# Mixing attention units two of a kind, one slot on, in a four-layer grid network

## What is computed

```python
def _L2_conv_ref(x, wq, bq, wk, bk, wv, bv):
    xf = x.reshape(B, N, C)          # N = 1024, C = 128; q and k have 16 channels
    q = xf @ wq + bq
    k = xf @ wk + bk
    v = xf @ wv + bv
    attn = jax.nn.softmax(jnp.einsum('bnd,bmd->bnm', q, k), axis=-1)
    out = jnp.einsum('bnm,bmc->bnc', attn, v)
    return out.reshape(B, H, W, C) + x
```

## Time and profile before

| | us |
|---|---|
| median of 3 runs | 4534.51 (4533.5 to 4537.09) |
| profiled execution, its own time | 4535.49 |
| its span, first to last instruction | 4533.4 |
| mean granted clock of TensorE, share of full speed | 0.986 |

### The profile page before, as it was taken

How to read it: one execution, slowest core, us unless ns; L and a number is a source line. 1 busy time by engine, 2 the same in 40 slices (tenths; PEclk the granted TensorE clock), 3 DMA queues, 4 the chain that set the end, 5 groups by cost and what they waited for, 6 DMA issues and landing times.

```text
span 4533.4 us, 56308 instructions
## 1 busy us (share of the span) xinstructions
PE 4349.7 (96%) x16776; PEld 2252.3 (50%) x16776; DVE 3476.5 (77%) x6544; ACT 2842.2 (63%) x5235; POOL 2267.5 (50%) x3972
## 2 busy tenths in 40 slices
PE   6989996999999999999999999999999999999996
PEld 2446654444444444444444444444444444446754
DVE  5988876777777777777777777777777775898876
ACT  1323322788888888888888888888888884333321
POOL 4654431455555555555555555555555556564431
PEclk9999998899999999999999999999999999999998
DMA  9869419111111122222211111112222221679429
GB/s 165 96 69 109 94 28 67 42 59 60 60 60 56 55 69 70 70 71 71 67 61 59 60 60 60 55 55 67 69 71 71 71 65 33 64 85 121 86 37 47
DMA packets 482495, 309.68 MB, mean 68 GB/s; under 512 B 420624, under 2 KB 432272, under 8 KB 482192
## 3 DMA queue, kind: packets, MB, share of 16 engines
q1 hardware_dynamic: 479088, 305.03, 35.2%
q10 hardware_dynamic: 3104, 1.06, 0.2%
HBM read 137.21 MB, written 135.27 MB: 60 GB/s over the span
## 4 chain that ended last, share of the span: by engine, by line
PE 64%; DVE 9%; ACT 8%; issue 8%; POOL 7%; SPq 2%; DMA 0%; DVEq 0%; POOLq 0%; ACTq 0%
PE psum L1158 14%; PE psum L1078 7%; PE psum L1129 6%; PE psum L1068 6%; PE psum L1092 5%; POOL probs_low L597 4%; PE psum L1142 3%; PE psum L1166 3%; PE psum L1164 3%; PE psum L1163 3%; PE psum L1201 3%; PE psum L1179 3%; PE psum L1188 3%; ACT shared L972 3%; PE psum L1087 3%
## 5 line engine op out<-in xcount | busy, mean ns | idle before, releaser
L597 POOL TENSOR_TENSOR probs_low<-shared,probs_high 128x512 fp32r<-128x512 f32 x1024 | 1307.4, 1277 | 1300.2 <-DVE probs_high L907 1300.2
L869 DVE TENSOR_REDUCE top<-psum 128x1 f32<-128x1024 f32 x1024 | 1253.9, 1225 | 616.1 <-PE psum L1142 615.8
L977 ACT ACTIVATE psum<-psum,top 128x1024 f32<-128x1024 f32 x1024 | 1114.9, 1089 | 279.6 <-DVE top L869 279.6
L972 ACT ACTIVATE shared<-psum 128x512 f32<-128x512 f32 x2048 | 1108.3, 594 | 258.9 <-PE psum L1129 258.8
L1158 PE MATMUL psum<-shared 128*128 128x512 f32 x2048 | 1123.6, 630 | 0.9 <-issue 0.5
L962 ACT ACTIVATE shared<-psum,b_col 128x320 f32<-128x320 f32 (+10 forms) x744 | 413.6, 567 | 1009.5 <-PE psum L1078 995.0
L588 POOL TENSOR_TENSOR shared<-arena 128x32 f32<-128x32 f32 (+6 forms) x1230 | 588.7, 509 | 764.8 <-PE psum L1078 725.2
L1163 PE MATMUL psum<-probs_high,v_high 128*128 128x512 f32 x1024 | 811.5, 792 | 0.0
L1068 PE MATMUL psum<-arena,w_own 128*128 128x320 f32 (+12 forms) x1672 | 539.5, 450 | 21.6 <-DVE w2wy L713 20.8
L1078 PE MATMUL psum<-shared,w_sum 128*128 128x320 f32 (+10 forms) x1488 | 523.3, 474 | 28.7 <-POOL shared L588 13.7
L1129 PE MATMUL psum<-q,k 64*128 64x512 f32 x2048 | 513.2, 497 | 0.3 <-ACT shared L972 0.3
(11 more groups left out here) (115 smaller groups left out, 4455.1 us busy)
## 6 DMA issues: line engine op xcount, KB each, us to landing
layer_out<-x SPq DMA_DIRECT2D x128, 512.0 KB, 2.6
x<-layer_out SPq DMA_DIRECT2D x124, 512.0 KB, 3.3
q<-q SPq DMA_DIRECT2D x256, 128.0 KB, 2.3
arena<-layer_out SPq DMA_DIRECT2D x63, 241.5 KB, 2.4
arena<-x_cells SPq DMA_DIRECT2D x6, 1520.0 KB, 12.3
layer_out<-arena SPq DMA_DIRECT2D x6, 1520.0 KB, 21.1
arena<-layer_out SPq DMA_DIRECT2D x6, 1520.0 KB, 10.9
y_cells<-arena SPq DMA_DIRECT2D x6, 1520.0 KB, 21.4
```

The source lines that it names most:

```text
L597: nc.gpsimd.tensor_tensor(probs_low[n % 2][:], probs[u % PROBS], probs_high[n % 2][:], ALU.subtract).then_inc(probs_split, 1)
L869: nc.vector.reduce_max(top[i % 2][:, m:m + 1], rows_ps[m % 2][:], AX_X, negate=True).then_inc(row_max, 1)
L972: nc.scalar.activation(probs[u % PROBS], keys_ps[u % 2], ACT.Exp).then_inc(probs_ready, 1)
L977: nc.scalar.activation(rows_ps[m % 2][:], rows_ps[m % 2][:], ACT.Exp, bias=top[i % 2][:, m:m + 1], accum_out=total[i % 2][:, m:m + 1]).the ...
```

## The change

Units are mixed two of a kind. The units of an even slot (u // 2 even) are mixed in fp32, both; those of an odd slot in three passes, both. Mixing is still one slot behind, so TensorE mixes in fp32 in odd slots and in passes in even slots. In a pass slot the four products with high parts come first, then the two with low parts. The casts and subtractions of a pair stand together in the odd slots. Value tiles are dealt out anew so that `v` (fp32) and `v_high`, `v_low` hold what their units need. `project_keys` moves from slot 6, before the mix, to slot 5, behind it; the query split on VectorE and the swap on SP from slot 7 to slot 0 of the next turn, `low_values` to slot 4; the shift's last three operations before its rounding go to a function of their own in slot 3 (`log_corrections`), the rest of `shift_values` to slot 4. No product, cast or subtraction is added or removed. The core of the diff:

```diff
+def in_passes(u):
+    return u // 2 % 2 == 1
...
+def split_index(i, u):
+    return UNITS // 2 * i + 2 * (u // 4) + u % 2
...
@@ SP
+                    if s == 0:
+                        swap_queries(j + 2)
...
-                    if s == 7:
-                        swap_queries(j + 3)
@@ GpSimd
-                split_probs(j, 2 * s + 1)
                 if s == 2:
                     log_sums(j + 1)
                 if s == 3:
+                    log_corrections(j + 1)
+                if s == 4:
                     shift_values(j + 1)
+                if in_passes(2 * s):
+                    split_probs(j, 2 * s)
+                    split_probs(j, 2 * s + 1)
@@ VectorE
-            row_maximum(j + 1 + (s + 6) // MT, (s + 6) % MT)
+            if s == 0:
+                split_queries(j + 2)
             if s == 2:
                 guess_log(j + 1)
-            if s == 3:
+            if s == 4:
                 low_values(j + 1)
+            row_maximum(j + 1 + (s + 6) // MT, (s + 6) % MT)
             if s == 5:
                 take_shift(j + 1)
             if s == 6:
                 split_keys(j + 3)
-            if s == 7:
-                split_queries(j + 3)
-            round_probs(j, 2 * s + 1)
+            if in_passes(2 * s):
+                round_probs(j, 2 * s)
+                round_probs(j, 2 * s + 1)
@@ ScalarE
             exponentials(j, 2 * s)
-            exponentials(j, 2 * s + 1)
             if s == 2:
                 shrink_sums(j + 1)
+            exponentials(j, 2 * s + 1)
@@ TensorE
+        def mix_whole(i, first):
...
+            for u in (first, first + 1):
                 pe.wait_ge(probs_ready, UNITS * i + u + 1)
-                nc.tensor.matmul(mix_ps, v[i % 2][:, t], probs[u % PROBS], start=(m == 0), stop=False
+                nc.tensor.matmul(mix_ps, v[i % 2][:, value_rows(u)], probs[u % PROBS], start=(u % MT == 0), stop=False
                                  ).then_inc(mixed, 1)
...
+        def mix_passes(i, first):
...
+            for u in (first, first + 1):
+                pe.wait_ge(probs_rounded, split_index(i, u) + 1)
+                nc.tensor.matmul(mix_ps, v_high[i % 2][:, value_rows(u)], probs_high[u % 2][:], start=False, stop=False)
+                nc.tensor.matmul(mix_ps, v_low[i % 2][:, value_rows(u)], probs_high[u % 2][:], start=False, stop=False)
+            for u in (first, first + 1):
+                pe.wait_ge(probs_split, split_index(i, u) + 1)
+                nc.tensor.matmul(mix_ps, v_high[i % 2][:, value_rows(u)], probs_low[u % 2][:], start=False,
+                                 stop=(u % MT == MT - 1)).then_inc(mixed, 1)
...
-            if s == 6:
-                project_keys(j + 3)
             if s == 7:
                 project_queries(j + 3)
-            for u in (2 * s - 2, 2 * s - 1):
-                mix(j + u // UNITS, u % UNITS)
+            i, first = j + (2 * s - 2) // UNITS, (2 * s - 2) % UNITS
+            if in_passes(first):
+                mix_passes(i, first)
+            else:
+                mix_whole(i, first)
+            if s == 5:
+                project_keys(j + 3)
```

More of the change, by code:

```diff
@@ L311, in tile, with value_tiles @@
     return slice(m * P, (m + 1) * P)
+def in_passes(u):
+    return u // 2 % 2 == 1
+def split_index(i, u):
+    return UNITS // 2 * i + 2 * (u // 4) + u % 2
+def value_tiles(h):
+    return [g * MT // 2 + p for p in range(h, MT // 2, 2) for g in range(2)]
 def queries_at(g, h):
@@ L594, in split_probs @@
             if is_job(i):
-                n = UNITS // 2 * i + u // 2
+                n = split_index(i, u)
                 pool.wait_ge(probs_rounded, n + 1)
@@ L614, in log_sums, with log_corrections @@
             nc.gpsimd.tensor_tensor(slope[:], slope[:], excess[:], ALU.mult).then_inc(log_turn, 1)
+        def log_corrections(i):
+            if not is_job(i):
+                return
+            turn = LOG_TURNS * i + 6
+            pool.wait_ge(log_turn, turn)
+            nc.gpsimd.tensor_scalar(slope[:], slope[:], -0.5, None, ALU.add).then_inc(log_turn, 1)
+            nc.gpsimd.tensor_tensor(log_sum[:], log_sum[:], excess[:], ALU.subtract).then_inc(log_turn, 1)
+            pool.wait_ge(log_turn, turn + 2)
+            nc.gpsimd.tensor_tensor(slope[:], slope[:], square[:], ALU.mult).then_inc(log_turn, 1)
         def shift_values(i):
@@ L621, in shift_values @@
             high, low = shift[i % 2][:, 0:MT], shift[i % 2][:, MT:2 * MT]
[L622 to L626, removed]
             pool.wait_ge(log_turn, turn + 3)
@@ L903, in round_probs @@
             if is_job(i):
-                n = UNITS // 2 * i + u // 2
+                n = split_index(i, u)
                 dve.wait_ge(probs_ready, UNITS * i + u + 1)
-                positive(dve, mixed, 2 * (n - 2) + 2)
+                positive(dve, mixed, UNITS * i + u - 3)
                 nc.vector.tensor_copy(probs_high[n % 2][:], probs[u % PROBS]).then_inc(probs_rounded, 1)
@@ L967, in exponentials @@
                 act.wait_ge(keys_ready, UNITS * i + u + 1)
-                if u % 2 == 0:
+                if in_passes(u):
+                    positive(act, probs_split, split_index(i, u) - 1)
+                else:
                     positive(act, mixed, UNITS * i + u - PROBS + 1)
-                else:
-                    positive(act, probs_split, UNITS // 2 * i + u // 2 - PROBS // 2 + 1)
                 nc.scalar.activation(probs[u % PROBS], keys_ps[u % 2], ACT.Exp).then_inc(probs_ready, 1)
@@ L1145, in row_energies, with value_rows @@
             mm.then_inc(rows_ready, 1)
-        def mix(i, u):
+        def value_rows(u):
+            return tile(2 * (u % MT // 4) + u % 2)
+        def mix_whole(i, first):
             if not is_job(i):
                 return
-            h, m = u // MT, u % MT
-            if u == 0:
+            h = first // MT
+            if first == 0:
                 pe.wait_ge(v_ready, 2 * i + 2)
-            if m == 0:
+            if first % MT == 0:
                 positive(pe, out_ready, 2 * i + h)
-            t = tile(m // 2)
-            if m % 2 == 0:
+            for u in (first, first + 1):
                 pe.wait_ge(probs_ready, UNITS * i + u + 1)
-                nc.tensor.matmul(mix_ps, v[i % 2][:, t], probs[u % PROBS], start=(m == 0), stop=False
+                nc.tensor.matmul(mix_ps, v[i % 2][:, value_rows(u)], probs[u % PROBS], start=(u % MT == 0), stop=False
                                  ).then_inc(mixed, 1)
[L1160 to L1167, removed]
+        def mix_passes(i, first):
+            if not is_job(i):
+                return
+            for u in (first, first + 1):
[6 more added lines that the diff above has]
+                                 stop=(u % MT == MT - 1)).then_inc(mixed, 1)
         def project_keys(i):
@@ L1199, in project_values @@
                 pe.wait_ge(v_ready, 2 * i + 1)
-            for m in range(MT // 2):
-                mm = nc.tensor.matmul(misc_ps[:, tile(m)], x[i % DEEP][:, tile(h * MT // 2 + m)],
+            for m, t in enumerate(value_tiles(h)):
+                mm = nc.tensor.matmul(misc_ps[:, tile(m)], x[i % DEEP][:, tile(t)],
                                       wv_sb[job_layer(i)][:], start=True, stop=True)
```

## The result

The changed kernel takes 4620.05 us (median of 4 runs, 4617.66 to 4621.55), the kernel before 4534.58 (4 runs): 1.0187 times as long, 95% interval 1.0175 to 1.0200. Forecast were 4616 us and a range of 4585 to 4655.

The account below looks back on a forecast made before the run. TensorE was taken as the bound, busy 2966 of 2984 us in the attention stage. All terms were 0 except +81 us for the query product's wait: 4534.5 + 81 = 4616 us, range 4585 to 4655.

Parts of the forecast that it names:

- Array work, term 0: TensorE's mixes: a fp32 slot of 2.58 and a pass slot of 2.26 sum to 4.84, as before.
- rival 2: TensorE's three-pass group straight after row-tiled products: entering costs nothing instead of 0.20, so 4541 us, no change; chance 0.07.
- The turned shift, term 0: Slot 5: the late shift's 0.20 wait goes, but the mix then waits for the first half's output; no net gain.
- My bound for it, 0.20: Slot 5's turned shift: term 0 was given bounds of 0 and -0.20 us a job.
- The key product and the query product behind it, +81 us: Slot 7's query product waits for VectorE's key split: 0.65 us a job in 125 jobs, 81 us.
- Splits in pairs, term 0: Paired casts and subtractions on VectorE and GpSimd end before TensorE's low-part product needs them; no cost.
- the 0.42 to spare: Pass slots: second low part there 1.43 into the slot, its product starting at 1.91; 0.42 left after 0.06 to pass on.
- The prediction's 0.32 for this loss: GpSimd's first subtraction: by a full lock, the second cast, 0.10 ahead of it, delays it by 0.32.
- Rival 1: Subtractions start first and block VectorE's second cast; last product waits 0.13 in slots 2 and 4: 4649 us, chance 0.08.
- the 0.10 by which a subtraction might grow: GpSimd's split beside VectorE's cast loses 0.10, judged by an 8-column product that took 0.30 where its neighbour took 0.20.
- Rival 3: TensorE's first pass after fp32 really takes 0.40 more; eight such entries a job go: some 4206 us, chance 0.06.
- Rival 4: No wait before slot 7's query product, as TensorE reaches it late for another reason: 4510 to 4535 us, chance 0.05.

Follow-up runs that it names:

- the first experiment: The changed kernel with the key product put back in slot 6, before the mix: 4530.28 us, ratio 0.9994 to the kernel before.
- the second: The kernel before with only the key product moved to slot 5, behind the mix: 4593.48 us, ratio 1.0134.
- the third experiment: The changed kernel with VectorE splitting the keys ahead of slot 6's row maximum: 4573.86 us, ratio 1.0087.
- the fourth experiment: The kernel before with the key product in slot 5 before the mix and the turned shift in slot 6: 4497.80 us, ratio 0.9924.

## Why the prediction was right

*Array work, term 0: right.* A slot in passes was put at 2.26 and is 2.25, one in fp32 with values at 2.58 + 0.89 = 3.47 and is 3.47. The entry that the trace of before didn't show, three passes straight after row-tiled products, costs 0.19 to 0.20: 0.43 for the first pass against 0.24 for the next in the chain above. That rules out rival 2 (entry free, 4541 us): pass slots of 2.06 would be needed.

*The turned shift, term 0: right, and its reason now tested.* It starts 1811.35 - 1810.69 = 0.66 into slot 5 with no wait, and the mix behind it 0.91 into the slot, as predicted, because of the output. The late shift had been a wait that stood in front of another of nearly the same end: taking it away moved 0.01 or so. Only covering the output gained, 0.26 a job. My bound for it, 0.20, was short: it left 0.07 of the 0.27 in the job's sum to the shift's own product, which costs 0.02.

*The key product and the query product behind it, +81 us: right.* k_ready at 3.51 plus 0.05 into slot 6, the query product due at 2.93: 0.63 where 0.65 was forecast, 80 us in 125 jobs. The first experiment shows that without this move there is no loss, the second that the move by itself makes 60 us of it, as much as its slot lengths say.

*Splits in pairs, term 0: right in the dense stage.* GpSimd's pair in slot 3 of one job ran from 1807.38 to 1810.01, 1.57 into slot 4, and its product started at 1810.37, 1.92 into the slot; no slot of the dense stage waited for it beyond 0.02. But the 0.42 to spare was mis-sized, at both ends. The pair was to end 1.43 into the slot and ends at 1.57: 0.11 of that is what the first subtraction loses to the cast (1.38 for 1.27), and without that a pair is 2.63 - 0.11 = 2.52 long where the sum had 2.49. The prediction's 0.32 for this loss, by a full lock, was too much: the subtraction starts 0.26 before the cast's end, and some 0.14 of its length passes beside the cast. And the product's start is not when its input is due, since its weights are loaded ahead of it, from 1.70 on. The latest end that the dense stage still bore was 1.74 in one slot, which was 2.28 long instead of 2.25; an end at 2.05 made 2.55. So the cover was about 0.2 and not 0.42. The term of 0 stands with either; in the third experiment 0.9 us later on VectorE were enough to turn it into 0.30 a job. Rival 1 (the casts block the splits, 4649 us) needed the subtraction to come first, and none of the 1024 casts starts inside a subtraction. The row behind the 0.10 by which a subtraction might grow was read rightly: the small product `slope<-slope,square` took 0.30 in the 125 jobs in which a cast stood beside it, and 0.20 in the three in which none did. Wrong was that no cast had run beside a subtraction so far: the two long ones named above were in the trace of before.

*Rival 3 (the change of type is saved, 4206 us): wrong,* as the steps of the chain had said. After the change no three-pass unit of the dense stage follows fp32 work directly, the long record of 0.79 is gone there, and in the first experiment a job, with fp32 slots and pass slots in place of mixed ones, is as long as it was (23.395 against 23.389). A record's length beside an overlapping neighbour is no cost. Nor is a single distance between starts, as I had put it ahead of the prediction: in the trace of before L1163 is recorded from 0.03 behind its fp32 neighbour and L1164 0.63 after that, while the chain charges L1163 with 0.23. The distance from slot to slot is what counts.

*Rival 4 (no wait): wrong* by the rows of the query product, which waits in every job.

The measured time is 4 us over the forecast: 2 to 3 of them in the last three jobs, which I had put within 1 together with the fill. There pairs end 2.1 to 2.5 into a pass slot in four of the slots, each of which is 0.3 to 0.7 longer for it.

## What to carry to other kernels

When a step is moved on the engine that sets the pace, look for whoever waits for its result, and count the time from the event that gates the consumer's input (here a row maximum that is ahead in VectorE's queue), not from the moved step itself: the key product started 0.66 into slot 6 and now starts 1.00 ahead of that slot, yet its result is ready 3.51 into it both times, while its reader has come forward. Work that stands between a producer on another engine and its consumer is cover: before it is shortened or moved, subtract what goes from the time at which the consumer is reached, and see whether the input is still there first. And where two waits end at the same instruction, removing the first gains next to nothing until something independent is put over the second: there the same product, put in front of the mix, gained 36 us.

## What was not expected of the hardware

- A product on 16 columns (the turned shift) costs the array 0.02 us between row-tiled and full-array work, though its weights alone are recorded with 0.09 (slot 6 of the fourth experiment, 2.43 against 2.41).
- A wait before the last product of a slot costs more than it seems from the product's start. In the third experiment the subtraction ended at 2.05 into slot 0, only 0.1 behind the 1.93 to 1.95 at which the product starts elsewhere, and the slot grew by 0.30. The wait holds the product's weight load, which otherwise starts at 1.70, under the product before it; here load and product both start at 2.10, and the product's record is 0.49 long instead of 0.39. Counted from 1.74, the latest end that was borne, the 0.31 are there.
